# An RWKV block with a gated feed-forward: the first gate/up units in column parts between the layer-norm tiles

## The reference

```python
xn  = layernorm(x)                        # no scale, no shift, eps 1e-5
k   = xn @ Wk.T ;  r = xn @ Wr.T          # v is r as well
y   = wkv_scan(-exp(time_decay), time_first, k, r)   # numerically stable recurrence over time
a   = (sigmoid(r) * y) @ Wo.T
f   = (silu(xn @ (wg/127).T) * (xn @ (wu/127).T)) @ (wd/127).T     # integer weights, 3072 hidden
out = x + a + f
```

## Time and profile before

| | us |
|---|---|
| median of 3 runs (lowest, highest) | 1359.59 (1359.39, 1359.64) |
| the profiled execution's own time | 1359.52 |
| its span on the slowest core (core 3); the other cores | 1358.0; 1355.6 to 1357.8 |
| TensorE busy | 1334.7 (98%) |
| VectorE busy | 674.6 (50%) |
| ScalarE busy | 396.5 (29%) |
| GpSimd busy | 35.2 (3%) |

### The profile page before, as it was taken

The page is one execution under the profiler, slowest core; times in us unless marked ns, Lnnn a source line. Parts: engine busy times, 40 slices in busy tenths (PEclk is TensorE's granted clock), DMA queues, the critical chain, the costliest instruction groups (busy, mean ns, idle before and its releaser), DMA issues.

```text
span 1358.0 us, 17854 instructions; the slowest of 8 cores (1355.6 to 1358.0 us)
## 1 busy us (share of the span) xinstructions
PE 1334.7 (98%) x6208; PEld 606.6 (45%) x6208; DVE 674.6 (50%) x1101; ACT 396.5 (29%) x663; POOL 35.2 (3%) x70
## 2 busy tenths in 40 slices
PE   4999999999999999999999999999999999999999
PEld 2444444444444444444444444444444444444444
DVE  4666666515952288323873238721487215672211
ACT  5554545312331233212332123221233212221100
POOL 0111111000000000000000000000000000000000
PEclk9999999999999999999999999999999999999999
DMA  9699989953554544545545444544455443334411
GB/s 231 144 183 196 209 163 181 204 142 120 167 144 148 168 137 135 147 150 176 125 117 163 155 156 124 143 152 156 150 143 126 155 155 124 94 102 164 153 47 55
DMA packets 90376, 200.41 MB, mean 148 GB/s; under 512 B 32816, under 2 KB 35888, under 8 KB 90160
## 3 DMA queue, kind: packets, MB, share of 16 engines
q1 hardware_dynamic: 55584, 167.81, 39.0%
q0 software_dynamic: 9360, 25.17, 12.5%
q10 hardware_dynamic: 25344, 6.29, 2.5%
HBM read 184.56 MB, written 33.55 MB: 161 GB/s over the span
## 4 chain that ended last, share of the span: by engine, by line
PE 98%; DMA 2%; SPq 0%; issue 0%; DVE 0%; DVEq 0%; POOLq 0%
PE ps L309 33%; PE ps L313 33%; PE ps_o L327 24%; PE ps_o L334 8%; DMA ring<-w_gu 1%; DMA x_buf<-x_tm 1%; PE ps L291 0%; SPq L170 0%; DVE xres L556 0%; DVEq L555 0%; POOLq L255 0%
## 5 line engine op out<-in xcount | busy, mean ns | idle before, releaser
L309 PE MATMUL ps<-xn,ring 128*128 128x512 bf16 x2048 | 485.5, 380 | 4.1 <-DMA ring<-w_gu 3.9
L313 PE MATMUL ps<-xn,ring 128*128 128x512 bf16 x2048 | 484.7, 379 | 0.0
L549 DVE SCALAR_TENSOR_TENSOR h_act<-ps,silu 128x512 bf16<-128x512 f32 x192 | 132.5, 690 | 438.4 <-PE ps L313 427.5
L327 PE MATMUL ps_o<-wd_bf,h_act 128*128 128x512 bf16 x1536 | 342.0, 379 | 0.0
L309 PEld LDWEIGHTS ps<-xn,ring 128*128 128x128 bf16 x2048 | 200.5, 98 | 246.1 <-issue 6.2
L313 PEld LDWEIGHTS ps<-xn,ring 128*128 128x128 bf16 x2048 | 200.7, 98 | 242.6 <-issue 1.7
L420 ACT ACTIVATE silu<-ps 128x512 f32<-128x512 f32 x192 | 114.6, 597 | 452.7 <-PE ps L309 452.4
L327 PEld LDWEIGHTS ps_o<-wd_bf,h_act 128*128 128x128 bf16 x1536 | 150.3, 98 | 181.3
L334 PE MATMUL ps_o<-wo_bf,outp 128*128 128x512 bf16 x512 | 120.9, 379 | 0.0
L402 ACT ACTIVATE den<-den 128x512 f32<-128x512 f32 x64 | 40.3, 630 | 260.1 <-DVE den L537 259.9
L556 DVE TENSOR_TENSOR xres<-xres,ps_o 128x512 f32<-128x512 f32 x64 | 44.0, 688 | 87.0 <-PE ps_o L334 86.4
(11 more groups left out here) (40 smaller groups left out, 319.1 us busy)
## 6 DMA issues: line engine op xcount, KB each, us to landing
ring<-gu_bfd SPq DMA_DIRECT2D x144, 512.0 KB, 3.3
ring<-kr_bfd SPq DMA_DIRECT2D x48, 512.0 KB, 3.9
xres<-x_tm SPq DMA_DIRECT2D x64, 256.0 KB, 5.5
out_tm<-xres SPq DMA_DIRECT2D x64, 256.0 KB, 4.7
x_buf<-x_tm SPq DMA_DIRECT2D x28, 512.0 KB, 6.4
ring<-w_gu POOLq DMA_DIRECT2D x24, 512.0 KB, 11.3
gu_bfd<-ring SPq DMA_DIRECT2D x24, 512.0 KB, 7.4
ring<-w_kr POOLq DMA_DIRECT2D x8, 512.0 KB, 7.4
```

The costliest lines, as they stand in the source:

```text
L309: ins = te.matmul(bank(kind, idx, 0), w[:, gc * D:(gc + 1) * D], xn[c % 2][:, gc, :], start=(gc == 0), stop=(gc == G - 1))
L313: ins = te.matmul(bank(kind, idx, 1), w[:, C + gc * D:C + (gc + 1) * D], xn[c % 2][:, gc, :], start=(gc == 0), stop=(gc == G - 1))
L327: te.matmul(ps_o[i % 2], h_act[c % 2][:, hg * TC + tt * D:hg * TC + (tt + 1) * D], wd_bf[:, half, hg * 512:(hg + 1) * 512], start=(hg == 0 ...
L549: ve.scalar_tensor_tensor(out=h_act[c % 2][:, hg * TC:(hg + 1) * TC], in0=bank("gu", i, 1), scalar=1.0 / (127.0 * 127.0), in1=silu[i % 3], ...
```

## The change

The arithmetic is the same; the order in the prologue and the banks differ.

- TensorE: `tr` writes to the banks `ps_o` instead of taking a pair. `SLOTS` holds only units. A new `gu_part` does the columns of some token tiles of a `gu` unit: 16 matmuls of 128 columns per tile (or of 384 for three tiles), into the same two banks.
- The order becomes tile 0, gu0 on tile 0, tile 1, gu0 on tile 1, tile 2, gu0 on tile 2, tile 3, gu1 on tiles 0 to 2, gu0 and gu1 on tile 3, gu2, then tiles 4 to 7 with parts of gu3 and gu4 between them, gu5, kr0, kr1, and from gu6 on as before. Before, kr0 stood between gu2 and gu3.
- SP: tiles 0 to 3 are loaded first; tiles 4 and 5 wait until the second weight block has landed, 6 and 7 until the third. The loads of `xres` stand behind them.
- POOL: the first weight load waits for no tile, the second and third for tile 1, the fourth for tile 6.
- ScalarE copies both halves of tile 0. ScalarE and VectorE work tile by tile, and gates 0 and 1 stand before tile 5.

```diff
-SLOTS = [("tr", l0) for l0 in range(NT)]
-SLOTS += [("gu", 0), ("tr", 4), ("gu", 1), ("tr", 5), ("gu", 2), ("tr", 6), ("tr", 7), ("kr", 0)]
+SLOTS = [("gu", i0) for i0 in range(6)] + [("kr", 0), ("kr", 1)]
...
-                for l in range(2 * NX):
+                for l in range(NX):
                     x_load(l)
...
+                sy.wait_ge(*loaded(1))
+                x_load(NX)
+                x_load(NX + 1)
+                sy.wait_ge(*loaded(2))
+                x_load(NX + 2)
+                x_load(NX + 3)
...
-                gp.wait_ge(sem["xl3"], 16)
                 for n in range(NS):
+                    if n == 1:
+                        gp.wait_ge(*x_landed(1))
+                    if n == 3:
+                        gp.wait_ge(*x_landed(6))
...
+                def gu_part(i, t0, t1):
+                    c = GU[i][0]
+                    if t0 == 0:
+                        acquire("gu", i)
+                        te.wait_ge(*loaded(RING_AT[("gu", i)]))
+                    w = ring[RING_AT[("gu", i)] % R]
+                    for m in range(2):
+                        for gc in range(G):
+                            if m == 0 and gc % 4 == 0:
+                                evacuated(NT * c + t1 - 1, gc // 4)
+                            ins = te.matmul(bank("gu", i, m)[:, t0 * D:t1 * D],
+                                            w[:, m * C + gc * D:m * C + (gc + 1) * D],
+                                            xn[c][:, gc, t0 * D:t1 * D],
+                                            start=(gc == 0), stop=(gc == G - 1))
+                        if t1 == NT:
+                            ins.then_inc(sem["t_u" if m else "t_g"], 1)
...
                 att_max(0)
-                for s in range(1, 2 * G):
+                att_scan(0)
+                att_den(0)
+                att_max(1)
+                att_out(0)
+                for s in range(2, 2 * G):
```

More of the change, by code:

```diff
@@ L278, in acquire, with evacuated @@
                     pk, pi = SLOTS[q - 3]
[L279 to L285 removed]
+                    te.wait_ge(sem["v_h" if pk == "gu" else "v_zA"], pi + 1)
+                def evacuated(l, k):
+                    if l == 0 or k == 0:
+                        te.wait_ge(sem["s_ev"], l + 2 if l else k + 1)
+                    else:
+                        te.wait_ge(sem["v_ev"], l)
                 def tr(l):
[L288 removed]
                     te.wait_ge(sem["s_xt"], l + 1)
                     for cb in range(G):
[L291 removed]
+                        if l >= 1 and cb % 4 == 0:
+                            evacuated(l - 1, cb // 4)
+                        ins = te.matmul(ps_o[cb // 4][:, (cb % 4) * D:(cb % 4 + 1) * D],
                                         xt[l % 2][:, cb * D:(cb + 1) * D], ident, start=True, stop=True)
@@ L296, in xn_ready @@
                     if c < 2:
[L297 to L298 removed]
+                        evacuated(NT * c + NT - 1, 0)
+                        evacuated(NT * c + NT - 1, 1)
                     else:
@@ L338, in _ @@
                 te.wait_ge(sem["g_id"], 1)
-                for l in range(NT):
-                    tr(l)
-                xn_ready(0)
-                proj("gu", 0, 0, "t_g", "t_u")
+                tr(0)
+                gu_part(0, 0, 1)
+                tr(1)
+                gu_part(0, 1, 2)
+                tr(2)
+                gu_part(0, 2, 3)
+                tr(3)
+                gu_part(1, 0, 3)
+                gu_part(0, 3, 4)
+                gu_part(1, 3, 4)
+                proj("gu", 2, 0, "t_g", "t_u")
                 tr(4)
-                proj("gu", 1, 0, "t_g", "t_u")
+                gu_part(3, 0, 1)
                 tr(5)
-                proj("gu", 2, 0, "t_g", "t_u")
+                gu_part(4, 0, 1)
+                gu_part(3, 1, 2)
                 tr(6)
+                gu_part(4, 1, 2)
+                gu_part(3, 2, 3)
                 tr(7)
-                proj("kr", 0, 0, "t_k", "t_r")
-                xn_ready(1)
-                for s in range(1, 2 * G):
+                gu_part(4, 2, 3)
+                gu_part(3, 3, 4)
+                gu_part(4, 3, 4)
+                proj("gu", 5, 1, "t_g", "t_u")
+                for s in range(2):
+                    proj("kr", s, s, "t_k", "t_r")
+                for s in range(2, 2 * G):
                     for i in range(3 * s, 3 * s + 3):
@@ L396, in ln_ev @@
                     sc.wait_ge(sem["t_tr"], l + 1)
-                    sc.copy(out=xn[c % 2][:, 0:4, t * D:(t + 1) * D],
-                            in_=bank("tr", l, 0).rearrange("p (k t) -> p k t", t=D)).then_inc(sem["s_ev"], 1)
+                    for k in range(2 if l == 0 else 1):
+                        sc.copy(out=xn[c][:, 4 * k:4 * k + 4, t * D:(t + 1) * D],
+                                in_=ps_o[k].rearrange("p (k t) -> p k t", t=D)).then_inc(sem["s_ev"], 1)
                 def att_rec(a):
@@ L448, in _ @@
                 gate(0)
+                gate(1)
+                ln_rstd(5)
                 ln_ev(4)
+                ln_xt(5)
+                ln_rstd(6)
+                ln_ev(5)
                 ln_xt(6)
-                gate(1)
-                ln_ev(5)
+                ln_rstd(7)
+                ln_ev(6)
                 ln_xt(7)
+                ln_ev(7)
                 gate(2)
-                ln_ev(6)
-                ln_ev(7)
+                gate(3)
+                gate(4)
+                gate(5)
                 att_exp(0)
-                for s in range(1, 2 * G):
+                att_rec(0)
+                att_exp(1)
+                for s in range(2, 2 * G):
                     for i in range(3 * s, 3 * s + 3):
```

84 lines of the change are left out of this document (34 added, 50 removed).

## The result

The changed kernel takes 1364.49 us (median of 7 runs) against 1359.5 us of the kernel before on the same chip: ratio 1.0035, 95% interval 1.0023 to 1.0047. It is **slower by 5.0 us, 0.35%**; forecast were 1361.0 us and a range of 1358.6 to 1365.0, "no change" with 0.68 and "slower" with 0.27. The time lies in the range, 0.5 us under its upper end, and is more above the kernel before than the 2.7 us that the prediction called measurable: what came is the case that it had called "slower". In some executions one die is granted a lower clock and the time is longer (the highest of these seven is 1458.81); ratios and all medians from here on leave these out, by which the change is at 1364.4.

The account below looks back on a forecast made before the run. TensorE was taken as the bound (98% of the chain), only its early waits winnable. gu6 0.0, gu8 +0.9, narrow matmuls +0.3, handoffs +0.3 give +1.5 on 1359.52, hence 1361.0 us; range 1358.6 to 1365.0.

Parts of the forecast that it names:

- gu6 at the same time 0.0: Start of the seventh gate/up unit: forecast 56.2 us against 56.18 before, so the net is nothing.
- signs of being wrong: gu6 before 54 or after 59, tile 4's copy not behind a table load, or half-pace matmuls behind 35 us.
- late data: Rival: tile 4 or the first block lands late; 3 us late about 1363, 6 us 1365.5; chance 0.15.
- Chunk 0: Tiles 0 to 3 with gu0 parts between transpositions: about 4.8 us won by the end of tile 4's transposition at 32.6.
- The wait of 2.4: TensorE idle from 32.6 to 35.0 before gu3 on tile 4, for ScalarE's copy behind table load, Ln and Exp.
- Loads: Start: first block lands at 12, second near 16, tile 4 at 21, needed at 22.4; covered by about 1 us.
- The pace falls back: Rival: TensorE's clock drops in chunk 1's waits, +3.8 to +5.2 us, 1364.8 to 1366.2; chance 0.10.
- The pace rises early: Rival: TensorE reaches full pace during the parts from 17.2 on; gu6 about 54.5, 1359.3 us; chance 0.12.
- The tile loop: Chunk 1, tiles 6 and 7: loop of 2.9 us against TensorE's 2.25, so 0.6 idle for each.
- gu8: Ninth gate/up unit waits for kr1's pair because kr0 and kr1 follow each other: +0.9 us.
- Narrow matmuls: Matmuls of 128 columns at 0.056 each, +0.3 us taken; rival: 0.098 apart by weight loads, 3.7 (high end), 1364.4; chance 0.05.
- Table loads: ScalarE's three loads near 27.6, 32.5 and 43, 1.28 us each; rival: dearer, about +5, 1366, chance 0.03.

Follow-up runs that it names:

- Experiments 2 and 3: The change with tiles 4 to 7 asked for when the first block has landed: 1364.5 us; the same with the third block behind tile 5: 1364.6 us.
- experiment 5: The change with ten idle matmuls of 512 columns filling TensorE's wait ahead of gu3's first part: 1364.2 us, ratio 1.0038 to before.
- experiment 6: The change with kr0 and kr1 taken apart, gu5 between them: 1363.4 us, ratio 1.0033 to before.
- experiment 12: The change with chunk 1 apart, w_dn's blocks later and statistics staggered, but without the parts of gu0 and gu1: 1362.0 us, ratio 1.0020 to before.
- experiment 8: The change with chunk 1's transpositions between whole or half units, its Ln and Exp before the first gate, kr0 and kr1 apart, loads restaged: 1359.5 us, ratio 1.0004 to before.

## Why the prediction came out as it did

The mechanism was right, the sum too small by 3.5 us, and the price forecast as "nothing" ("gu6 at the same time 0.0") is the term that was wrong: gu6 came 2.9 us later on core 3, and 3.5 in the mean. Two of the prediction's own signs of being wrong came true, gu6 after 59 (59.06 on core 3) and matmuls behind 35 us at half pace. That the time is still inside the range is partly luck: its upper end stood for the clock or late data at its near end, and what filled the gap was several small terms.

- *Chunk 0.* First part at 13.59 against 12.8, since the block landed 11.3 us after its request at 2.0. The transpositions at 15.25, 18.79 and 22.33 (forecast 15.4, 18.9, 22.3) and the end of tile 4's at 32.8 (32.6) are right, and with them 4.6 of the 4.8 us won up to there.
- *The wait of 2.4.* It was in its place and for its reason, a copy behind table load, Ln and Exp: 3.22 on core 3 and three others, 2.63 on four. 0.8 short.
- *Loads.* "Covered, by about 1 us" was wrong: the second block, behind which tile 4 is asked for, landed at 18.3 and not near 16, and VectorE began on tile 4 at 24.24, 1.8 us later than the 22.4 at which it was needed. Experiments 2 and 3 and core 5 of the change show that this wasn't the loss ahead of gu6: the wait is 2.4 to 2.6 with the tile in time.
- *The pace falls back*, a rival with 0.10, happened on seven of eight cores. It cost 0.8 (core 2 against 3; experiment 5 gives 0.7), not the 3.8 to 5.2 that I worked out for it (with 1.4 per tile, where 4.5 less 2.9 is 1.6): the clock was back at 39, within one tile, and ScalarE's loop hid part of the slow one. Its chance was too low, since I had only asked whether the trace showed a gap behind a fast stretch; it showed none, which speaks for neither.
- *The pace rises early*, a rival with 0.12, happened on cores 0 and 2, where the parts at 17.6 and 18.1 already ran at full pace. Core 0 was the first at gu6 (57.43, 1.2 ahead of the mean), core 2 won 0.3: for them too the wait for the copy of tile 4 was 3.22. That the waits bound this gain was right.
- *The tile loop.* 3.06 (44.39 less 41.33) against 2.9 per tile, two waits of 0.58 (0.6) and one of 0.94 (0.8) before gu5. With the end of tile 4's transposition (+0.2), the wait (+0.8), the clock (+0.8), the loop (+0.3) and gu5 (+0.1) gu6 is 2.3 later than the 56.8 that includes the handoffs and narrow matmuls. That closes the sum to 0.1.
- *gu8* +1.1 against +0.9, confirmed by experiment 6.
- *Narrow matmuls.* 48 in 2.93, 0.17 of it the modelled tail, is 0.058 each: 0.2 in all for the last group, as taken. The 98 ns of the earlier trace rows isn't their spacing. The Trainium skill (TensorE: Matmul & The Clock Gate, Back-to-back issue gap) has 81 ns; the trace disagrees. By the steps of the high end these 81 ns would also have given about 1.3 and not the 1.9 that the prediction names.
- *Table loads* at 28.35, 33.67 and 45.69, each 1.28: as taken, up to 2.7 later.
- Left out, and no run gives a reason for either: from the last addition to the end of the span it is 2.8 now and was 2.4; another 0.25 appears between gu8 and that addition, in no wait of size.

The miss of 3.5 is thus, within rounding, 2.3 (gu6), 0.2 (gu8), 0.25, 0.4 and the 0.2 by which the medians differ more than the spans (4.8). I had compared with core 3 of before, its slowest: 56.18 there, 55.1 in the mean. Over all cores gu6 moved by 3.5, not 2.9.

The change thus holds two halves of opposite sign. Parts of gu0 between the transpositions are worth about 3.2 us by the estimate of experiment 12; the order of chunk 1, with parts of gu3 and gu4 taken up where ScalarE still has to switch tables between gates and layer norms, costs more than that (gu6 4.9 later than in experiment 8, which changes that order alone ahead of gu6, but for the staging of the loads).
